# Layer 1's first eight maxima moved into the last two expert tiles of layer 0, and its second batch's queries spread over steps 1 to 4

## The chip, the cores and the metric

The kernel runs on one NeuronCore of a Trainium2 chip. Its engines are TensorE (PE in the profile; its weight loads are PEld), VectorE (DVE), ScalarE (ACT), GpSimd (POOL) and SyncE (SP, which here only issues DMAs). The trace counts a float32 matmul as two instructions. Each works through its own instructions in order and waits on semaphores for the others. The metric is the device time of one execution in microseconds; lower is better.

## The reference, cut to what matters

Two layers of cross attention and a mixture of experts, in float32, for x of 2 x 512 x 256 and a context of 2 x 1024 x 256:

```python
x = x + xattn0(layernorm(x), ctx, ctx, mask0)       # 16 heads of 16
x = x + experts0(layernorm(x))                      # top 1 of 8, 256 -> 512 (gelu) -> 256, cosine routing
x = x + xattn1(layernorm(x), ctx, ctx, mask1)       # q, k, v are each layer-normed after their projection
x = x + experts1(layernorm(x))                      # shared + top 2 of 7, 256 -> 704 -> 256
# in xattn1:
q = layer_norm(query @ Wq, gq, bq); k = layer_norm(key @ Wk, gk, bk); v = layer_norm(value @ Wv, gv, bv)
weights = softmax(q @ k.T / sqrt(16) + bias)        # per head, per batch element
out = weights @ v
```

The masks leave only the last 256 keys to be attended to in the rows that matter, so the fast way of the kernel works on 256 keys.

## The kernel before, in words

**Attention.** The work of a layer is eight steps n: batch element n // 4, four of the 16 heads (group n % 4). Each step has eight units of scores (`pe_scores`, units i = 0 to 7): two 32 x 128 by 256 matmuls into one bank of PSUM, head i % 4 in its own 32 rows of the array, queries of half i // 4. VectorE takes the row maxima of each unit (`dve_top`, L956) into NM. When the eight are done, TensorE turns NM (`pe_turn_max`, L783), VectorE adds it to the queries (`dve_add_max`, L962), so that the weights come out with their maximum taken off. Then TensorE computes eight units of weights, transposed (`pe_weights`, L774), ScalarE takes their Exp (L1084), TensorE multiplies with the values (`pe_outputs`, L795, two halves), and two steps later turns the outputs (`pe_turn_out`, L808), which VectorE divides (`dve_divide`). The maxima run ahead of the weights: while step n's weights are made, units 4 to 7 of step n + 1 and 0 to 3 of step n + 2 are scored. A step has four gaps with two units of weights and two of scores each; beside each gap stands a list of other jobs (`pe_beside`, `dve_beside`, `act_beside`).

**PSUM.** Scores go round banks 0 to 2 (m, freed by VectorE), weights and the jobs beside round banks 3 to 5 (e, freed by ScalarE), banks 6 and 7 are claimed by name (`claim`, `taken`). The order of uses is a table (`ring_uses`, `BESIDE_M`, `BESIDE_E`, `bank_uses`).

**Layer 0's experts.** Sixteen tiles of 128 tokens (`ffn0_pe`, L1603 up, L1614 down, L1616 bias), in the order: turn of the next tile's rows (L1591), up(i), mid(i), down(i - 1), beside(i); after the last tile down(15). Up goes to banks 0 and 1 in turn, the turned rows to bank 2, down to banks 3 and 4. ScalarE does Gelu (L1644) and takes the outputs out (`take_y`, L1635), SP stores them to DRAM; GpSimd gathers them back into token order.

**Before layer 1's first step.** For the first batch element: combine the gathered rows into x (L994), the statistics of the layer norm (L395 to L408: moments, their aggregation, an inverse root in small steps), normal rows (x1_0, by ScalarE in beside(12)), their turn (`turn_batch`, beside(13)), the projection to queries (`project_batch`, L364, beside(14)), the statistics and norms of these (q1_0, L430 and L434), then behind the expert tiles the turns by heads (`turned_heads`, L349) in `second_pe`, which ScalarE takes with scale and bias (`queries_out`, L624), and then `pe_first(1)`: units 0 to 7 of step 0 and 0 to 3 of step 1, while VectorE does the maxima. Behind the last expert tile every engine has a branch (`fork`) that reads whether any expert got more rows than its main tiles hold.

**The second batch element's queries.** VectorE combines and takes the statistics of x1_1 between the maxima of `pe_first(1)` (`queries_begun`), ScalarE norms them before its first Exp, TensorE turns them in step 0, gap 0, and projects in gap 2; statistics of q1_1 in step 1 between the maxima, norms at step 1, gap 3, then one turn by heads at gap 3 of each of steps 1 to 4.

## Time and profile before

| | us |
|---|---|
| median of 3 runs (545.52 to 547.08) | 546.33 |
| the profiled execution | 548.11 |
| its span | 546.9 |
| TensorE busy | 504.9 (92%) |
| VectorE busy | 261.6 (48%) |
| ScalarE busy | 207.3 (38%) |
| mean granted TensorE clock | 0.967 of full |

In the time of the span, layer 0's attention runs to about 140, its experts to 219.6, layer 1's attention to about 325, the shared expert to about 389, the routed experts to the end. The profile's slices of the granted clock are below full in two places: at about 125 to 132 and from 218 to 276.

### The profile page before, as it was taken

Reading aid. Unit: us, or ns where it says so; the run is one execution under the profiler, and the core shown is the slowest. Engines: PE = TensorE matmul, PEld = TensorE weight load, DVE = VectorE, ACT = ScalarE, POOL = GpSimd, SP = SyncE. Lnnn points to the kernel's source line nnn. Section 1 sums busy time; section 2 is a strip of 40 time slices with the busy share of each in tenths; the row PEclk is TensorE's granted clock in tenths of the full one; section 3 lists DMA queues with packets and bytes.
Section 4 is the critical chain, followed back from the end, with each engine's and each line's share of the span. In section 5 each row is a group of like instructions: output and inputs, shape, how many; then the busy total and the mean of one; then the engine's idle time right before and its main releaser. Section 6 shows DMA issues by size and latency. Waiting matters only on the chain.

```text
span 546.9 us, 8791 instructions
## 1 busy us (share of the span) xinstructions
PE 504.9 (92%) x3285; PEld 373.3 (68%) x3285; DVE 261.6 (48%) x789; ACT 207.3 (38%) x425; POOL 82.2 (15%) x108
## 2 busy tenths in 40 slices
PE   2999999999889999679699998999999999999995
PEld 1456555645778999546356435656799999999994
DVE  5567798673337364365577826161322222222220
ACT  2434645462346653225466662220122222222221
POOL 2400700002102110200000000017212122212222
PEclk9999999997999999859899999999999999999999
DMA  8500005997113230380000012009786677666712
GB/s 299 188 1 0 2 1 164 369 373 224 59 38 104 72 97 20 99 296 1 0 2 2 1 39 77 1 10 362 269 282 201 202 238 248 211 200 220 251 13 33
DMA packets 42435, 72.06 MB, mean 132 GB/s; under 512 B 3405, under 2 KB 33037, under 8 KB 42384
## 3 DMA queue, kind: packets, MB, share of 16 engines
q1 hardware_dynamic: 33648, 60.65, 32.5%
q0 software_dynamic: 4336, 6.75, 5.6%
q10 hardware_dynamic: 4400, 4.01, 2.3%
q8 instruction: 29, 0.48, 0.3%
q14 instruction: 22, 0.18, 0.1%
HBM read 56.88 MB, written 14.51 MB: 131 GB/s over the span
## 4 chain that ended last, share of the span: by engine, by line
PE 57%; DVE 5%; DMA 3%; issue 2%; ACT 1%; POOL 1%; POOLq 0%; ACTq 0%; DVEq 0%
PE PS L1817 16%; PE PS L1832 9%; PE PS L1726 6%; PE PS L764 4%; PE PS L774 4%; PE PS L1737 3%; PE PS L1614 3%; PE PS L1603 3%; PE PS L795 2%; DVE W L956 2%; DMA VR<-scratch_rows 1%; PE PS L364 1%; PE PS L349 1%; PE PS L333 1%; PE PS L808 1%
## 5 line engine op out<-in xcount | busy, mean ns | idle before, releaser
L956 DVE TENSOR_REDUCE W<-PS 128x2 f32<-128x512 f32 x128 | 84.7, 687 | 41.3 <-PE PS L764 40.6
L1817 PE MATMUL PS<-PR,W 128*128 128x128 f32 x836 | 96.5, 275 | 0.0
L1817 PEld LDWEIGHTS PS<-PR,W 128*128 128x128 f32 x836 | 94.9, 192 | 0.1
L764 PE MATMUL PS<-W 32*128 32x256 f32 x512 | 85.7, 432 | 3.1 <-issue 1.6
L774 PE MATMUL PS<-W 32*128 32x512 f32 x256 | 84.3, 672 | 0.7 <-ACT W L1084 0.7
L764 PEld LDWEIGHTS PS<-W 32*128 32x128 f32 x512 | 56.4, 201 | 18.5 <-DVE W L956 9.0
L1832 PE MATMUL PS<-W,PR 128*128 x228 | 52.5, 380 | 0.8 <-ACT PR L2461 0.8
L2512 POOL DMA_INDIRECT out<-PR,slots x19 | 29.6, 1560 | 128.6 <-ACT PR L2461 125.4
L1084 ACT ACTIVATE PR<-PS 128x512 f32<-128x512 f32 x64 | 34.9, 595 | 30.8 <-PE PS L774 30.6
L1832 PEld LDWEIGHTS PS<-W,PR 128*128 128x128 f32 x228 | 41.9, 190 | 6.1 <-issue 1.2
L1084 ACT ACTIVATE W<-PS 128x512 f32<-128x512 f32 x64 | 34.7, 595 | 24.0 <-PE PS L774 24.0
L1853 DVE TENSOR_TENSOR PR<-PR,PS 128x512 f32<-128x512 f32 x19 | 13.1, 688 | 59.8 <-PE PS L1817 59.8
L1726 PE MATMUL PS<-XT,W 128*128 128x512 f32 x88 | 40.1, 596 | 0.0
L774 PEld LDWEIGHTS PS<-W 32*128 32x128 f32 x256 | 26.0, 191 | 19.5 <-issue 6.7
L1603 PE MATMUL PS<-PR,W 128*128 128x128 f32 x256 | 31.2, 275 | 0.0
L1614 PE MATMUL PS<-W,PR 128*128 128x256 f32 x128 | 30.4, 381 | 0.0
L1603 PEld LDWEIGHTS PS<-PR,W 128*128 128x128 f32 x256 | 29.9, 192 | 0.1
L1726 PEld LDWEIGHTS PS<-XT,W 128*128 128x128 f32 x88 | 16.2, 190 | 16.5 <-issue 16.1
L1644 ACT ACTIVATE PR<-PS,b1c 128x128 f32<-128x128 f32 x64 | 18.2, 366 | 23.8 <-PE PS L1603 23.8
L1614 PEld LDWEIGHTS PS<-W,PR 128*128 128x128 f32 x128 | 23.1, 190 | 2.6
L1566 POOL DMA_INDIRECT scratch_rows<-CT,posi x8 | 7.8, 969 | 113.5 <-DVE posi L1530 111.4
L1737 PEld LDWEIGHTS PS<-W,PR 128*128 128x128 f32 x96 | 18.1, 190 | 8.7 <-issue 4.5
(260 smaller groups left out, 625.5 us busy)
## 6 DMA issues: line engine op xcount, KB each, us to landing
W<-in_rguT SPq DMA_DIRECT2D x19, 1408.0 KB, 6.1
W<-in_L_ffn_W SPq DMA_DIRECT2D x16, 512.0 KB, 9.6
W<-in_rdT SPq DMA_DIRECT2D x5, 768.0 KB, 9.5
W<-in_mask SPq DMA_DIRECT2D x3, 1024.0 KB, 14.3
scratch_rows<-W SPq DMA_DIRECT2D x1, 2860.0 KB, 14.8
VR<-scratch_rows SPq DMA_DIRECT2D x19, 130.0 KB, 5.3
scratch_x<-W SPq DMA_DIRECT2D x1, 2048.0 KB, 14.1
PR<-scratch_x SPq DMA_DIRECT2D x16, 128.0 KB, 2.2
```

The lines of the kernel that those rows point to most:

```text
L764: m = pe.matmul(PS[:, bank, q * FK:(q + 1) * FK], QT[r:r + 32, g, c:c + 128], KT[r:r + 32, g, b * FK:(b + 1) * FK], start=True, stop=True)
L774: pe.matmul(PS[:, bank, :], KT[r:r + 32, g, b * FK + kb * 128:b * FK + (kb + 1) * 128], QT[r:r + 32, g, 512 * b:512 * (b + 1)], start=True ...
L956: dve.tensor_reduce(NM[:, s % 2, q:q + 2, c], PS[:, m_bank(use), :].rearrange("p (q n) -> p q n", q=2), AX, ALU.max).then_inc(sem("m_free" ...
L1084: act.activation(PX[s % 2][:, HEADS_W[k], :], PS[:, e_bank(use), :], ACT.Exp).then_inc(sem("e_free"), 1)
L1603: m = pe.matmul(PS[:, i % 2, j * 128:(j + 1) * 128], W[:, o:o + 128], XS0[:, i % 2, k, :], start=(k == 0), stop=(k == 1))
L1614: pe.matmul(PS[:, bk, 0:D], HT0[:, i % 2, j, :], W[:, o:o + D], start=(j == 0), stop=False)
L1644: act.activation(HT0[:, i % 2, j, :], PS[:, i % 2, j * 128:(j + 1) * 128], ACT.Gelu, bias=b1c[:, c:c + 1]).then_inc(sem("gelu"), 1)
L1726: m = pe.matmul(PS[:, 2 * (n % 2) + w, :], W[:, k * 2 * F1 + o:k * 2 * F1 + o + 128], XT[:, k, 512 * b:512 * b + 512], start=(k == 0), sto ...
L1737: m = pe.matmul(half(4 + t // 2, t), HS[:, n % 2, t * 128:(t + 1) * 128], W[:, o:o + D], start=(j == 0 and t % 2 == 0), stop=(j == NJ1 - 1 ...
L1817: m = pe.matmul(PS[:, bank, j * 128:(j + 1) * 128], W[:, o:o + 128], XS[:, r % 2, k, :], start=(k == 0), stop=(k == 1))
L1832: m = pe.matmul(PS[:, 6, 0:D], HT[:, r % 2, j, :], W[:, bass.ds(slot * SLOT + o, D)], start=(j == 0), stop=(j == NJ1 - 1))
L2512: ins = pool.indirect_dma_start(out, off, YO[:, r % 2, :], None, compute_op=ALU.add)
```

## The change

- **Inside the expert tiles** (`fast_...`, `ffn0_...`): VectorE norms two of the four rows of x1_0 and ScalarE two, in tile 11; the turn moves to beside(12), the projection to mid(13), the norms of q1_0 into tile 13, the four turns by heads to beside(14) (two) and mid(15) (two). The up matmuls swap banks 0 and 1 (`up_bank`).
- **First eight maxima:** units 0 to 7 of layer 1's step 0 are issued in pairs: in the middle of up(15), in the middle of down(14), in beside(15), in the middle of down(15). Units 0 to 3 of step 1 and the turned maxima follow the last tile, ahead of the branch.
- **Second batch's queries:** the combine runs in step 0 from gap 2; the statistics of x1_1 stand as one block before step 1's maxima; norms at step 1, gap 0; turn at gap 1; projection at gap 3; statistics of q1_1 in step 2, two pieces per maximum; its norms at step 3, gap 0; the turns by heads at step 3, gaps 0, 1 and 3, and step 4, gap 3.
- **Scores of steps 4 and 5:** units 0 to 3 of step 4, which need these queries, move from step 2 to step 3: none in step 2, gaps 2 and 3, and step 3, gap 0, then four in each of gaps 1, 2 and 3 of step 3; the turned maxima of step 4 move to the end of gap 3.
- The way for overfull experts (`again_...`, left out here) recomputes what the tiles now hold.

In the diff below many of the removed lines are left out; they stand in the functions printed above.

```diff
-    BESIDE_E = {(0, 5, 1): ["close0_0"], (0, 7, 1): ["rows0_0_0"], (1, 0, 0): ["x1_1_0"], (1, 0, 2): ["q1_1_0", "q1_1_1"]}
-    BESIDE_E.update({(1, 1 + g, 3): [f"q1t1_{g}"] for g in range(NG)})
+                (0, 7, 1): ["rows0_0_1"], (1, 1, 1): ["x1_1_1"]}
+    BESIDE_E = {(0, 5, 1): ["close0_0"], (0, 7, 1): ["rows0_0_0"], (1, 1, 1): ["x1_1_0"], (1, 1, 3): ["q1_1_0", "q1_1_1"],
+                (1, 3, 0): ["q1t1_0"], (1, 3, 1): ["q1t1_1"], (1, 3, 3): ["q1t1_2"], (1, 4, 3): ["q1t1_3"]}
+    def tops_of(l, n, gap):
+        if (l, n, gap) in ((1, 2, 2), (1, 2, 3), (1, 3, 0)):
+            return []
+        if (l, n) == (1, 3):
+            return [(4, i) for i in range(4 * gap - 4, 4 * gap)] if gap < 3 else [(5, i) for i in range(4)]
+        s, first = (n + 1, 4 + 2 * gap) if gap < 2 else (n + 2, 2 * gap - 4)
+        return [(s, i) for i in (first, first + 1) if s < STEPS]
...
         else:
+            if (n, gap) == (1, 1):
                 pe.wait_ge(sem("x1_rows"), 8)
                 turn_ring("x1_1", rows_for(0, 1))
+            elif (n, gap) == (1, 3):
                 pe.wait_ge(*e_freed("x1_1_0"))
                 pe.wait_ge(*m_freed("x1_1_1"))
                 for j in range(2):
                     project_half(e_claim(f"q1_1_{j}"), j, 2, 1).then_inc(sem("e_full"), 1)
+            elif (n, gap) == (3, 0):
+                pe.wait_ge(sem("q1_rows"), 4)
+                turned_heads(e_claim("q1t1_0"), RB[1], 0).then_inc(sem("e_full"), 1)
+            elif (n, gap) == (3, 1):
+                turned_heads(e_claim("q1t1_1"), RB[1], 1).then_inc(sem("e_full"), 1)
+            elif n in (3, 4) and gap == 3:
                 turned_heads(e_claim(f"q1t1_{n - 1}"), RB[1], n - 1).then_inc(sem("e_full"), 1)
...
+    def pe_pairs(l, n, gap):
+        tops = tops_of(l, n, gap)
+        if gap % 2:
+            pe_weights(l, n, 2 * gap)
+            pe_weights(l, n, 2 * gap + 1)
+            for s, i in tops:
+                pe_scores(l, s, i)
+            return
+        for k in range(2):
+            for s, i in tops[k:k + 1]:
+                pe_scores(l, s, i)
+            pe_weights(l, n, 2 * gap + k)
+        for s, i in tops[2:]:
+            pe_scores(l, s, i)
     def pe_step(l, n):
+        pe_pairs(l, n, 0)
         pe_turn_out(l, n - 2)
         pe_beside(l, n, 0)
+        pe_pairs(l, n, 1)
         pe_outputs(l, n - 1, 1)
         pe_beside(l, n, 1)
+        pe_pairs(l, n, 2)
+        if (l, n) != (1, 3):
+            pe_turn_max(l, n + 1)
         pe_beside(l, n, 2)
+        pe_pairs(l, n, 3)
+        if (l, n) == (1, 3):
+            pe_turn_max(l, n + 1)
         if n == STEPS - 1:
             pe_turn_out(l, n - 1)
         pe_outputs(l, n, 0)
...
+    def dve_step(l, n, v, late, pieces=1, since=0):
         for gap in range(4):
+            tops = tops_of(l, n, gap)
+            for k, (s, i) in enumerate(tops):
+                if gap == 1 and n > 1 and k == len(tops) - 1:
                     dve_divide(l, n - 2, v)
+                dve_top(l, s, i)
+                if gap >= since:
+                    for _ in range(pieces):
+                        next(late, None)
+            if gap == 1 and n > 1 and not tops:
+                dve_divide(l, n - 2, v)
+            if gap == (3 if (l, n) == (1, 3) else 2) and n + 1 < STEPS:
                 dve_add_max(l, n + 1)
...
     def act_beside(l, n, gap):
...
+            if (n, gap) == (1, 0):
+                act_x1(1)
+            elif (n, gap) == (1, 1):
                 act_xt_ring("x1_1", 1)
+            elif (n, gap) == (1, 3):
                 for j in range(2):
...
+            elif (n, gap) == (3, 0):
+                act.wait_ge(sem("stats"), NORMS[True]["q1_1"])
+                act.wait_ge(sem("wz"), 16)
+                for j in range(4):
+                    normal_act("q1_1", j, heads(RB[1][:, j, :]), by_head(RW[:, j, :])).then_inc(sem("q1_rows"), 1)
+                act_late_queries(0)
+            elif (n, gap) == (3, 1):
+                act_late_queries(1)
+            elif n in (3, 4) and gap == 3:
+                act_late_queries(n - 1)
             elif (n, gap) == (7, 1):
                 rows_taken_act(1, 0)
...
-    def ffn0_pe(tiles, beside, mid=lambda i: None):
+    def up_bank(i):
+        return (i + 1) % 2
...
+                if j == NJ0 // 2:
+                    half(i, "up")
                 for k in range(2):
                     o = expert(i) + k * F0 + j * 128
-                    m = pe.matmul(PS[:, i % 2, j * 128:(j + 1) * 128], W[:, o:o + 128], XS0[:, i % 2, k, :],
+                    m = pe.matmul(PS[:, up_bank(i), j * 128:(j + 1) * 128], W[:, o:o + 128], XS0[:, i % 2, k, :],
                                   start=(k == 0), stop=(k == 1))
             m.then_inc(sem("up"), 1)
...
             for j in range(NJ0):
+                if j == NJ0 // 2:
+                    half(i, "down")
                 o = expert(i) + 2 * F0 + j * D
...
                 ranks_pe(1).then_inc(sem("ranks"), 1)
+            elif i == 13:
+                pe.wait_ge(sem("wp_2"), 16)
+                project_batch("q1_0", "x1_0", 2, 0)
+            elif i == 15:
+                claim(7, "q1t0_2")
+                filled(7, turned_heads(7, RB[0], 2))
+                pe.wait_ge(*at(1, "qt", 1))
+                turned_heads(5, RB[0], 3).then_inc(sem("q_ps"), 1)
+        def first_maxima(i, part):
+            if (i, part) == (15, "up"):
+                pe.wait_ge(*at(1, "qt", 1))
+                pe.wait_ge(*at(1, "masked", 1))
+                pe.wait_ge(sem("gelu"), NJ0 * 15)
+                pe_scores(1, 0, 0)
+                pe_scores(1, 0, 1)
+            elif (i, part) == (14, "down"):
+                pe.wait_ge(sem("gelu"), NJ0 * 16)
+                pe_scores(1, 0, 2)
+                pe_scores(1, 0, 3)
+            elif (i, part) == (15, "down"):
+                pe_scores(1, 0, 6)
+                pe_scores(1, 0, 7)
         def beside(i):
...
-            elif i == 13:
+            elif i == 12:
                 pe.wait_ge(sem("x1_rows"), 4)
                 turn_batch("x1_0", rows_for(0, 0))
...
             elif i == 14:
+                taken(6, "q1_0")
+                taken(7, "q1_0")
+                turned_heads(5, RB[0], 0).then_inc(sem("q_ps"), 1)
+                claim(6, "q1t0_1")
+                filled(6, turned_heads(6, RB[0], 1))
+            elif i == 15:
+                pe_scores(1, 0, 4)
+                pe_scores(1, 0, 5)
+        ffn0_pe(MAIN, beside, mid, first_maxima)
+        pe.wait_ge(*at(1, "masked", 4))
+        pe.wait_ge(*at(1, "qt", 2))
+        taken(6, "q1t0_1")
+        taken(7, "q1t0_2")
+        pe_scores(1, 1, 0)
+        pe_scores(1, 1, 1)
+        pe_turn_max(1, 0)
+        pe_scores(1, 1, 2)
+        pe_scores(1, 1, 3)
         fork(pe, 0)
...
+        pe.wait_ge(sem("y_out"), TILES0)
+        pe.wait_ge(sem("vv1"), 4)
...
+            elif i == 10:
+                for n in range(3):
+                    dve.wait_ge(*at(1, "kt", n + 1))
+                    mask_keys(1, n)
             elif i == 11:
                 dve.wait_ge(sem("kept"), 16)
                 whole(combine(v, 0))
                 whole(statistics(v, "x1_0", rows_of(0)))
+                for j in range(2):
+                    normal_dve("x1_0", j, OB[:, 0, j, :], X[:, j, :]).then_inc(sem("x1_rows"), 1)
             elif i == 12:
+                dve_xt("x1_0", 0)
             elif i == 13:
                 raw = [half(6 + j // 2, j) for j in range(4)]
                 whole(statistics(v, "q1_0", raw, True, [full(6 + j // 2, "q1_0") for j in range(4)]))
+                dve.wait_ge(sem("pads"), 3)
+                normal_dve("q1_0", 2, heads(RB[0][:, 2, :]), by_head(half(7, 2))).then_inc(*v.up())
+                freed(7, normal_dve("q1_0", 3, heads(RB[0][:, 3, :]), by_head(half(7, 3))))
+            elif i == 14:
+                dve.wait_ge(*at(1, "kt", 4))
+                mask_keys(1, 3)
+            elif i == 15:
+                dve_first(1, nothing)
...
+            late = begun if s < 2 else queries_norm() if s == 2 else rows_early() if s == 6 else empty
+            if s == 0:
+                dve_step(1, s, v, late, 1, 2)
+                continue
+            if s == 1:
+                whole(late)
+            dve_step(1, s, v, late, 2 if s == 2 else 1)
             whole(late)
             if s == 5:
...
+            elif i == 11:
+                act.wait_ge(sem("stats"), NORMS[True]["x1_0"])
+                for j in (2, 3):
+                    normal_act("x1_0", j, OB[:, 0, j, :], X[:, j, :]).then_inc(sem("x1_rows"), 1)
             elif i == 12:
+                act_xt("x1_0", (6,), 0)
             elif i == 13:
+                act.wait_ge(sem("stats"), NORMS[True]["q1_0"])
+                act.wait_ge(sem("pads"), 3)
+                normal_act("q1_0", 0, heads(RB[0][:, 0, :]), by_head(half(6, 0))).then_inc(sem("q1_half"), 1)
+                freed(6, normal_act("q1_0", 1, heads(RB[0][:, 1, :]), by_head(half(6, 1))))
+            elif i == 14:
+                queries_out(1, 0, 5).then_inc(sem("qt"), 1)
+                act.wait_ge(*full(6, "q1t0_1"))
+                freed(6, queries_turned(1, 0, 1, 6))
+            elif i == 15:
+                act.wait_ge(*full(7, "q1t0_2"))
+                freed(7, queries_turned(1, 0, 2, 7))
+                act.wait_ge(*at(1, "q_ps", 2))
+                queries_turned(1, 0, 3, 5).then_inc(sem("qt"), 1)
```

## Rows read from the trace of the kernel before

**Rows 1.** The page's part 4: shares of the span in the chain, by engine.

```profile
PE 57%; DVE 5%; DMA 3%; issue 2%; ACT 1%; POOL 1%; POOLq 0%; ACTq 0%; DVEq 0%
```

**Rows 2.** The chain that ended last, 200 to 300: start, us, what.

```profile
210.67 3.46 PE PS L364 x16
...
219.58 2.22 issue
...
280.78 0.59 PE PS L349 x4
...
288.35 0.99 PE PS L795 x8
289.34 0.59 PE PS L349 x4
```

**Rows 3.** Windows: busy us (count) of PE, PEld, DVE, ACT, POOL; clock; DMA share, GB/s.

```profile
50.00:52.00 2.00, 1.94 (x18) 1.15 (x17) 1.98 (x5) 0.72 (x2) 0.00 (x0) 1.00 0.00 0
...
219.58:289.86 70.28, 56.85 (x378) 37.35 (x377) 41.59 (x100) 31.98 (x56) 4.00 (x6) 0.81 0.23 76
226.00:228.00 2.00, 1.27 (x13) 0.84 (x8) 1.49 (x3) 0.00 (x0) 0.95 (x1) 0.90 0.33 86
228.00:230.00 2.00, 2.00 (x12) 1.81 (x11) 1.35 (x3) 0.00 (x0) 0.00 (x0) 0.50 0.17 53
...
248.00:250.00 2.00, 2.00 (x20) 1.61 (x14) 1.30 (x3) 1.58 (x3) 0.00 (x0) 0.98 0.00 0
...
268.00:270.00 2.00, 0.23 (x1) 0.23 (x2) 0.00 (x0) 1.72 (x4) 0.00 (x0) 0.64 0.00 0
...
274.00:276.00 2.00, 2.00 (x16) 1.27 (x20) 0.39 (x2) 0.26 (x2) 0.00 (x0) 0.65 0.00 0
```

**Rows 4.** Timeline of TensorE: start, us, line, form, count, idle before it.

```profile
201.94 0.38 PE L1591 MATMUL PS<-ident,PR 128*128 128x128 f32 x2
...
225.38 1.15 PE L764 MATMUL PS<-W 32*128 32x256 f32 x12 [1.61 <-issue]
...
244.51 1.97 PE L333 MATMUL PS<-ident,W 128*128 128x128 f32 x8 [3.75 <-ACT W L434]
...
269.77 1.11 PE L349 MATMUL PS<-ident,W 128*128 128x128 f32 x4 [5.10 <-ACT W L434]
```

**Rows 5.** Timeline of VectorE.

```profile
195.02 1.66 DVE L994 SCALAR_TENSOR_TENSOR X<-W,gw,X 128x256 f32<-128x256 f32 x4
196.71 1.41 DVE L395 BATCH_NORM_STATS2 ST<-X 128x6 f32<-128x256 f32 x4
...
200.81 0.16 DVE L408 SCALAR_TENSOR_TENSOR NW<-MV,NW 128x4 f32<-128x4 f32 x1
...
217.82 1.00 DVE L430 TENSOR_SCALAR W<-PS,MV,NW 128x256 f32<-128x256 f32 x2
226.51 1.89 DVE L956 TENSOR_REDUCE W<-PS 128x2 f32<-128x512 f32 x3 [7.70 <-PE PS L764]
```

**Rows 6.** Timeline of ScalarE.

```profile
219.90 1.02 ACT L434 ACTIVATE W<-PS,NW 128x256 f32<-128x256 f32 x2
...
244.47 1.28 ACT L1084 ACT_TABLE_LOAD   x1
...
267.65 2.07 ACT L434 ACTIVATE W<-W,NW 128x256 f32<-128x256 f32 x4 [3.15 <-DVE NW L408]
```

**Rows 7.** Timeline of TensorE in layer 0's opening.

```profile
38.02 1.14 PE L764 MATMUL PS<-W 32*128 32x256 f32 x8
39.09 1.98 PE L344 MATMUL PS<-XT,W 128*128 128x512 f32 x4
```

**Rows 8.** Timeline of all engines, GpSimd's gathers and SP's last store.

```profile
220.03 0.32 SPq L1688 DMA_DIRECT2D scratch_y<-PR  x1
...
222.46 0.94 POOL L1675 DMA_INDIRECT W<-scratch_y,posi  x1 [29.33 <-DMA scratch_y<-PR]
...
226.20 0.95 POOL L1675 DMA_INDIRECT W<-scratch_y,posi  x1 [0.30 <-issue]
```

More of the change, by code:

```diff
@@ L271, in ring_uses @@
             for n in range(STEPS):
-                tops = [("top", l, n + 1, i) for i in range(4, 8)] + [("top", l, n + 2, i) for i in range(4)]
                 for gap in range(4):
-                    m += [top for top in tops[2 * gap:2 * gap + 2] if top[2] < STEPS]
+                    m += [("top", l, s, i) for s, i in tops_of(l, n, gap)]
                     m += BESIDE_M.get((l, n, gap), [])
@@ L1002, in queries_begun, with dve_first @@
         yield from statistics(v, "x1_1", rows_of(1))
-    def dve_first(l, beside, late=iter(())):
+    def dve_first(l, beside):
         for i in range(8):
@@ L1035, in dve_beside @@
         else:
-            if (n, gap) == (0, 0):
+            if (n, gap) == (1, 1):
                 dve_xt_ring("x1_1", 1)
@@ L1039, in dve_beside @@
                 rows_taken_dve(1, 0)
-    def dve_step(l, n, v, late):
+    def dve_step(l, n, v, late, pieces=1, since=0):
         for gap in range(4):
-            s, first = (n + 1, 4 + 2 * gap) if gap < 2 else (n + 2, 2 * gap - 4)
-            for i in (first, first + 1):
-                if s < STEPS:
-                    dve_top(l, s, i)
-                    next(late, None)
-                if gap == 1 and i == 6 and n > 1:
-                    dve_divide(l, n - 2, v)
-            if gap == 2 and n + 1 < STEPS:
+            tops = tops_of(l, n, gap)
+            for k, (s, i) in enumerate(tops):
+                if gap == 1 and n > 1 and k == len(tops) - 1:
+                    dve_divide(l, n - 2, v)
+                dve_top(l, s, i)
[5 more added lines that the diff above has]
+            if gap == (3 if (l, n) == (1, 3) else 2) and n + 1 < STEPS:
                 dve_add_max(l, n + 1)
@@ L1154, in act_beside @@
                                    ).then_inc(sem("e_free"), 1)
-            elif 1 <= n < 5 and gap == 3:
-                if n == 1:
-                    act.wait_ge(sem("stats"), NORMS[True]["q1_1"])
-                    act.wait_ge(sem("wz"), 16)
-                    for j in range(4):
-                        normal_act("q1_1", j, heads(RB[1][:, j, :]), by_head(RW[:, j, :])).then_inc(sem("q1_rows"), 1)
-                use = f"q1t1_{n - 1}"
-                act.wait_ge(*e_full(use))
-                queries_turned(1, 1, n - 1, e_bank(use)).then_inc(sem("e_free"), 1)
+            elif (n, gap) == (3, 0):
[8 more added lines that the diff above has]
+                act_late_queries(n - 1)
             elif (n, gap) == (7, 1):
@@ L1582, in expert, with ffn0_pe @@
         return (i % E0) * EXP0
-    def ffn0_pe(tiles, beside, mid=lambda i: None):
+    def up_bank(i):
+        return (i + 1) % 2
+    def ffn0_pe(tiles, beside, mid=lambda i: None, half=lambda i, part: None):
         def turn_x(i):
@@ L2094, in again_dve @@
         whole(statistics(v, "q1_0", [half(6 + j // 2, j) for j in range(4)], "again"))
+        dve.wait_ge(sem("again_xt"), 2 + NG)
+        turns = 2 + NG
+        for n in range(12):
+            g, i = n // 8, n % 8
+            if n == 10:
+                turns += 1
+                dve.wait_ge(sem("again_turned"), turns)
+                qt = QT[:, 0, 0:512]
+                dve.tensor_tensor(qt, qt, PS[:, 7, :], ALU.add).then_inc(sem("again_xt"), 1)
+            turns += 1
+            dve.wait_ge(sem("again_turned"), turns)
+            q, c = 2 * (i // 4), 32 * (i % 4) + ROW_MAX
+            dve.tensor_reduce(NM[:, g, q:q + 2, c], PS[:, 0, :].rearrange("p (q n) -> p q n", q=2), AX, ALU.max
+                              ).then_inc(sem("again_xt"), 1)
     def second_dve(v):
         empty = iter(())
-        late = queries_begun(v)
-        def beside(i):
-            if i > 2:
-                next(late, None)
         def queries_norm():
@@ L2110, in rows_early @@
             yield from dve_rows(1, 0)
-        dve_first(1, beside, late)
-        whole(late)
+        begun = queries_begun(v)
         for s in range(8):
-            late = queries_norm() if s == 1 else rows_early() if s == 6 else empty
-            dve_step(1, s, v, late)
+            late = begun if s < 2 else queries_norm() if s == 2 else rows_early() if s == 6 else empty
[5 more added lines that the diff above has]
+            dve_step(1, s, v, late, 2 if s == 2 else 1)
             whole(late)
@@ L2179, in fast_act @@
         ffn0_act(MAIN, beside)
-        act.wait_ge(sem("stats"), NORMS[True]["q1_0"])
-        for j in range(2):
-            ins = normal_act("q1_0", j, heads(RB[0][:, j, :]), by_head(half(6, j)))
-            if j == 0:
-                ins.then_inc(sem("q1_half"), 1)
-        freed(6, ins)
         fork(act, 2)
```

126 lines of the change are left out of this document (43 added, 83 removed).

## The prediction

> **What bounds the kernel now.** I read first the chain that ended last: TensorE holds 57% of the span [rows 1], so the kernel is bound by the order of TensorE's work and by what it waits for. The stretch that the diff touches lies between the end of layer 0's last expert tile (219.58, where the chain goes over into issue) and the first weights of layer 1's step 4 (289.9, right behind the turned heads at 289.34 [rows 2]). I then read the windows [rows 3]: 70.28 us at a mean granted clock of 0.81. A step at full clock takes 8.56 us (280.78 to 289.34 [rows 2]). So the four steps would be worth some 34 us, and the stretch holds twice that.
>
> TensorE's timeline shows why [rows 4]. It stands 2.22 us for the query norm and the branch [rows 2], 1.61 us for ScalarE to take the turned queries, 3.75 us for the norm of x1_1 (a four-row statistic that VectorE does between maxima, then 2.07 us of ScalarE [rows 6]), and 5.10 us for the norm of q1_1 in step 1. The granted clock falls from 1.00 to 0.50 (2.4 to 1.2 GHz) after the first two of these gaps and some small matmuls, at about 227.8, and returns at about 248.0; it falls again at about 268.7, four microseconds into the 5.10 us gap, and returns at about 275.3 [rows 3]. That is 27 us at half clock.
>
> The opening (12 maxima, 227 to 240) is bound half by VectorE (1.89 for three maxima [rows 5]) and half by the slow clock; nothing else lies beside it.
>
> **The change part by part.** Times below are on the trace's own axis.
>
> *First queries.* The norms of x1_0 are split (two on VectorE, two on ScalarE), the turn moves to tile 12, the projection to tile 13, the four turns of heads to tiles 14 and 15. TensorE's amount does not change; where the work stood after the tiles it now stands within them. Check of the cover: the statistics end at 200.97 (last instruction at 200.81 [rows 5]), two norms each on both engines until 202.0; TensorE asks at 201.94: nothing. The projection ended at 214.13 (210.67 + 3.46 [rows 2]) and VectorE's two norms at 218.82 (217.82 + 1.00 [rows 5]), 4.7 us later; until beside(14) TensorE now has down(12), a turn of x, up(14) and down(13), the same work as up(15) and the two downs after the projection now (214.13 to 219.58, 5.45) and 0.2 more: 5.7. Cost 0; if the cover is 1 us short it is 1 us. On ScalarE the Gelus of tile 14 start 0.7 us late; down(14) asks for them 4 us later. The masks move one to two tiles earlier into idle time of VectorE.
>
> *Eight maxima in pairs.* A pair of scores between full matmuls costs 1.07 us in layer 0 (38.02 to 39.09 [rows 7]) at full clock. Bounds: 0.77 (three scores took 1.15 at 225.38 [rows 4], two thirds of it) to 2.1 (half clock). I take 1.07, the same form. Four pairs 4.3, and 1.96 for the turned heads that before ran at 221.80: the tiles end at 219.58 + 6.3 = 225.9. VectorE's two maxima (1.29) hide under the half downs of 0.9 and the next pair. The ring of three banks gives each score its bank in time (score 7 wants the fourth maximum's, free at about 223.4, and asks at 224.4).
>
> *Opening.* Two pairs and the turned maxima: 2 x 1.07 + 0.59 = 2.7, so 228.6. The branch then costs TensorE about 0.85: before, the norm ends at 220.92 [rows 6] and TensorE starts at 221.80 (219.58 + 2.22 [rows 2]). VectorE's branch, hidden before under 7.70 idle [rows 5], is now open: its last maxima end at 229.9, it goes on at 230.8. Bounds for each branch: 0.05 to 2.2 (the whole gap). ScalarE's wait for the last store of y, now ahead of the first Exp: the take-out of tile 15 ends at 226.5, 2.4 us to landing (220.03 to 222.46 [rows 8]): 228.9, not late. The load of the Exp table (1.28 [rows 6]) may come after the first weights: 0 to 1.3; taken 1.3, and VectorE's lag hides part, so 0.8.
>
> *Step 0.* VectorE bounds it: 230.8 + 8 maxima at 0.65 in a run (5.2) + 0.7 for the added maxima + 1.66 for the four combines [rows 5] + 0.8 = 239.2. The gathers that these want are issued from 228.9 at 1.24 apart [rows 8], the fourth at 232.6; the fourth is asked for at about 238.5, and lateness is possible only if a gather takes over 5 us; 0 to 1 us, taken 0. TensorE finishes its step at 237.1. The weight loads on SP's queue wait for the same gathers and come 6 to 7 us later; they have 80 us before they are used, cost 0.
>
> *Step 1.* All of x1_1's statistic now stands as one block ahead of VectorE's maxima: 4.26 (196.71 to 200.97 [rows 5]), until 243.5. Behind it on VectorE wait the maxima of (2,4) to (2,7), and on those TensorE, whose ring is full at 239.4. It stands until 244.2, 4.8 us. ScalarE's norms run 243.5 to 245.6, later than its step-1 Exps 0 and 1, earlier than its 2 and 3. A gap of 4.8 has its like in the 5.10 gap, where the clock fell; so half clock from about 244 to 248 (from 244.51 it took 3.4 us to return, from 269.77 5.5 [rows 3, 4]): bounds 0 to 5.5 us low, 0 to 3 us of cost; taken 2.4. Outputs 1.95 and the turn of x1_1 1.97 at half clock, then two pair blocks, turned maxima, outputs (1.0) and the projection (3.46): 255.9. So step 1 costs 18.8 from 237.1.
>
> *Step 2.* It has four maxima where a steady step has eight. q1_1's statistic goes in two pieces per maximum. VectorE from 256.6: four maxima 2.8, four moments 1.5, aggregates and first steps 0.9, divide 0.7, giving 262.5 for the last maximum, where TensorE wants it at 260.6: 1.9 us of wait (bounds 0 to 3). The step ends at 265.0, 9.1 us.
>
> *Step 3.* The norm of q1_1 stands here: weights 0.9, turned outputs 0.6, then ScalarE's two Exps and 2.07 of norms: TensorE stands from 266.5 to 269.05, 2.55 us instead of 5.10. ScalarE must take the first turned group before score (4,0) may start (0.8; the last of four cost TensorE the gap of 1.61 [rows 4]). Then twelve maxima in three gaps bound VectorE: 12 x 0.68 + 0.67 divide + 0.69 = 9.6, from 271.0 to 280.6. So step 3 costs 15.6 against 8.56; its bounds are 12 (TensorE's own work and the wait) and 18 (a second fall of the clock).
>
> Step 4 begins at 280.6 instead of 289.9. From there the orders are the same, every later time moves along, and the load of the last weights is tied to step 7's end as before. Sum: +6.3 at the tiles, then 54.7 us (225.9 to 280.6) where 70.3 stood: 9.3 us gained. The profiled execution took 548.11 (span 546.9), so 538.8; the median of the runs is 1.8 below it, so **537.0**.
>
> One rule is weighed here. TensorE is busy for all of 228 to 230 with scores alone, and the clock stays at 0.50 [rows 3]; in layer 0's first step, as thin and also behind VectorE, it is 1.00 (50 to 52 [rows 3]). The Trainium skill (TensorE: Matmul & The Clock Gate, section A second HAM failure mode: psum-queue depth-cycling) says that short idle moments between groups of matmuls, as banks are waited for, can make the clock swing although no pause is long. By that rule steps 0 and 3 run low, which is rival B; by layer 0's row they do not.
>
> **The rivals.**
>
> *A, the lumps hide better.* The branch shows on neither engine, the clock stays at full through step 1, the ring lets step 2 run as TensorE's work: 1.7 + 2.4 + 1 less, so 533.7, median 532. For it: layer 0's first step at 1.00; the wait of 3.75 did not occur at full clock, so its limit is not seen. Against it: the fall inside the 5.10 gap.
>
> *B, the clock falls in the steps that VectorE paces.* From about 229 to 250 and in step 3. Step 0 then costs TensorE four pair blocks of 2.1, 2.0, 1.1 and 1.3 = 12.8 instead of 9.9 at VectorE's pace, +2.5; step 3's scores, outputs and turned heads, 4.2 at full clock, take 7: +2.8. Total 5.3, so 544.1, median 542.3. For it: 227.8 to 248.0 in this trace, with like work. Against it: between halves of expert tiles full matmuls stand, which is how layer 0 ran its first eight maxima [rows 7].
>
> *C, the other side.* One mechanism: having fallen at the branch, the clock never returns before step 4, because waits for VectorE break up each step. TensorE's work from 229.4 to 280.6 at full clock is 16 blocks of 1.07, 7 outputs of 0.99 (288.35 [rows 2]), 8 turns of 0.59, a turn of 0.99 and 3.46 = 33; at half 66, and with the two norm waits (about 7.4) 73 instead of 51.2: 22 more, 12.7 slower than before, 560.8, median 559. It decides from the point where over 9.3 us of extra time, so 19 us of that work instead of some 4, runs at half clock. For it: 20 us in a row now. Against it: the clock returned at 248.0 and at 275.3 within ordinary steps.
>
> **How the numbers follow.** Chances: forecast 0.45, A 0.18, B 0.26, C 0.05, and 0.06 for a wait that I have not seen and that eats the gain. A measurement here tells about 0.3%, 1.6 us, from no change. The bounds of the terms (pairs, branches, step 1's clock, step 2's wait, step 3) give the forecast's own case 533.5 to 541; to leave out no more than 2 in 10 the range takes A's centre and B's far side: 532 to 544. Faster: forecast, A, B and a little of the rest, 0.88; same 0.05; slower 0.07.
>
> **What would show it.** Right: the last expert tile's matmuls end at 225 to 227; TensorE's granted clock is 1.00 there; the gap before the turn of x1_1 is 3 to 5 us with VectorE's statistic in it; the gap before the first turned q1_1 heads is 2 to 3 us; step 4 begins at 278 to 284; everything behind is of the same length. Wrong: a gap ahead of beside(12) or beside(14) over 1 us (first queries not covered), half clock from 229 on (B, C), or a statistic of x1_1 that waits for its gathers.

## The result, and the profile after

| | us |
|---|---|
| kernel after, median of 8 runs (549.2 to 553.04) | 550.85 |
| kernel before, median of 8 runs (545.52 to 549.29) | 546.88 |
| ratio, 95% interval | 1.0072 [1.0047, 1.0098] |
| profiled execution of after, its span | 552.44, 551.2 |
| mean granted TensorE clock | 0.964 |

The change makes the kernel slower by 0.7%, 4.0 us. The prediction was 537.0 with a range of 532 to 544 and a chance of 0.88 for faster: wrong in sign. Three single runs below (two of fill3_table0, one of sooner_split) lie over 1.5% above the fastest of their kernel, with a lower mean clock, and the medians and ratios leave them out.

The chain of waits of after begins its shares with this line; TensorE holds 58% of the span where it held 57% [rows 1].

```profile
PE 58%; DVE 6%; ACT 2%; DMA 2%; issue 1%; POOL 1%; ACTq 0%; POOLq 0%; DVEq 0%
```

The two traces first have to be laid on one axis. In this window of unchanged code the kernel before ran at a mean clock of 0.58:

```profile
124.00:132.00 8.00, 8.00 (x43) 2.82 (x42) 2.74 (x17) 1.44 (x3) 0.00 (x0) 0.58 1.01 298
```

The windows of after follow: the window, TensorE's and its weight loads' busy time, that of VectorE, ScalarE and GpSimd, and behind them the mean granted clock, the share of the DMA engines and GB/s. The first is the same stretch at 1.00, so after's axis runs 8 x 0.42 = 3.4 us ahead from there on.

```profile
124.00:132.00 8.00, 8.00 (x54) 4.88 (x53) 4.79 (x23) 1.80 (x4) 2.22 (x3) 1.00 0.98 298
225.80:293.77 67.97, 59.45 (x308) 33.11 (x306) 35.21 (x89) 27.80 (x49) 3.82 (x6) 0.72 0.23 76
226.00:228.00 2.00, 1.54 (x13) 0.89 (x10) 1.98 (x4) 0.98 (x1) 1.51 (x2) 1.00 0.24 66
225.80:238.83 13.03, 11.61 (x61) 6.33 (x59) 8.14 (x15) 5.74 (x9) 3.60 (x4) 0.61 0.57 190
268.00:270.00 2.00, 0.02 (x1) 0.02 (x1) 0.00 (x0) 1.93 (x4) 0.00 (x0) 0.91 0.01 4
265.73:293.77 28.04, 24.83 (x104) 13.82 (x100) 9.12 (x15) 8.63 (x16) 0.00 (x0) 0.57 0.01 1
280.00:282.00 2.00, 2.00 (x13) 1.47 (x15) 0.00 (x0) 1.03 (x2) 0.00 (x0) 0.50 0.00 0
292.00:294.00 2.00, 2.00 (x16) 0.92 (x12) 0.00 (x0) 0.12 (x1) 0.00 (x0) 0.62 0.05 8
```

The window from the first weights to step 4 answers to the 0.81 window of [rows 3]: its clock is 0.72. TensorE's timeline gives the places (the steps begin at 225.80, 238.83, 256.57, 265.73 and 293.77):

```profile
212.19 1.14 PE L775 MATMUL PS<-W 32*128 32x256 f32 x8
...
222.69 1.14 PE L775 MATMUL PS<-W 32*128 32x256 f32 x8
223.76 0.66 PE L794 MATMUL PS<-ident,W 128*128 128x128 f32 x4
...
225.80 0.69 PE L785 MATMUL PS<-W 32*128 32x512 f32 x1
...
228.96 1.22 PE L785 MATMUL PS<-W 32*128 32x512 f32 x1 [1.42 <-ACT PR L1090]
...
238.83 0.51 PE L775 MATMUL PS<-W 32*128 32x256 f32 x1
...
244.30 1.12 PE L775 MATMUL PS<-W 32*128 32x256 f32 x4 [2.46 <-DVE W L963]
...
256.57 0.48 PE L775 MATMUL PS<-W 32*128 32x256 f32 x1
...
263.09 0.66 PE L794 MATMUL PS<-ident,W 128*128 128x128 f32 x4 [1.43 <-DVE W L963]
263.68 1.13 PE L785 MATMUL PS<-W 32*128 32x512 f32 x4
264.74 1.07 PE L806 MATMUL PS<-PR,VR 128*32 128x512 f32 x8
265.73 1.13 PE L785 MATMUL PS<-W 32*128 32x512 f32 x4
...
269.98 1.11 PE L360 MATMUL PS<-ident,W 128*128 128x128 f32 x4 [2.53 <-ACT W L445]
...
284.86 5.20 PE L775 MATMUL PS<-W 32*128 32x256 f32 x17
...
293.77 0.48 PE L775 MATMUL PS<-W 32*128 32x256 f32 x1
```

Step 3 is 28.04 us long against 15.6 forecast, at a mean clock of 0.57. VectorE, which was to bound it, is idle for long stretches there, as its own timeline of after shows (the number in brackets is the idle time before):

```profile
225.06 0.68 DVE L969 TENSOR_TENSOR W<-W,PS 128x512 f32<-128x512 f32 x1
225.66 2.60 DVE L963 TENSOR_REDUCE W<-PS 128x2 f32<-128x512 f32 x4
...
274.91 1.89 DVE L963 TENSOR_REDUCE W<-PS 128x2 f32<-128x512 f32 x3 [9.44 <-PE PS L775]
...
282.68 1.29 DVE L963 TENSOR_REDUCE W<-PS 128x2 f32<-128x512 f32 x2 [4.22 <-PE PS L775]
```

### The profile page after: what moved, and what is told of

Its sections match the earlier page's. It is cut to its first block, busy times and chain, and to the rows that moved or that the text cites. A ratio compares the mean times of both kernels' runs of the same rounds, so it can differ in the third digit from the quotient of the medians.

```text
span 551.2 us, 8794 instructions
## 1 busy us (share of the span) xinstructions
PE 512.9 (93%) x3285; PEld 374.8 (68%) x3285; DVE 263.7 (48%) x791; ACT 206.0 (37%) x423; POOL 82.6 (15%) x108
## 4 chain that ended last, share of the span: by engine, by line
PE 58%; DVE 6%; ACT 2%; DMA 2%; issue 1%; POOL 1%; ACTq 0%; POOLq 0%; DVEq 0%
PE PS L1838 17%; PE PS L1853 8%; PE PS L1747 6%; PE PS L775 5%; PE PS L785 4%; PE PS L1758 3%; PE PS L1635 3%; PE PS L806 3%; PE PS L1622 2%; DVE W L963 2%; PE PS L375 1%; PE PS L360 1%; PE PS L794 1%; DVE ST L406 1%; PE PS L344 1%
## 5 line engine op out<-in xcount | busy, mean ns | idle before, releaser
L775 PE MATMUL PS<-W 32*128 32x256 f32 x512 | 89.0, 437 | 4.3 <-DVE W L963 3.5
L785 PE MATMUL PS<-W 32*128 32x512 f32 x256 | 86.4, 682 | 2.2 <-ACT PR L1090 1.4
L775 PEld LDWEIGHTS PS<-W 32*128 32x128 f32 x512 | 57.5, 204 | 29.5 <-DVE W L963 14.1
L785 PEld LDWEIGHTS PS<-W 32*128 32x128 f32 x256 | 26.3, 195 | 15.4 <-issue 6.5
L1665 ACT ACTIVATE PR<-PS,b1c 128x128 f32<-128x128 f32 x64 | 18.2, 366 | 19.6 <-PE PS L1622 19.6
```

What stands on the lines that cost most here:

```text
L775: m = pe.matmul(PS[:, bank, q * FK:(q + 1) * FK], QT[r:r + 32, g, c:c + 128], KT[r:r + 32, g, b * FK:(b + 1) * FK], start=True, stop=True)
L785: pe.matmul(PS[:, bank, :], KT[r:r + 32, g, b * FK + kb * 128:b * FK + (kb + 1) * 128], QT[r:r + 32, g, 512 * b:512 * (b + 1)], start=True ...
L1665: act.activation(HT0[:, i % 2, j, :], PS[:, up_bank(i), j * 128:(j + 1) * 128], ACT.Gelu, bias=b1c[:, c:c + 1]).then_inc(sem("gelu"), 1)
```

## The experiments

Four kernels ran on one chip (kernel before there 548.21), four on a second (547.95), two on a third (549.28). Ratios are to the kernel before on the same chip; the kernel after itself was timed only against the 546.88 above, so it is compared with the others by ratio. The theory: step 3's thin work (scores alone, and a wait) holds the clock at half and is TensorE's own cost. The rivals: the fall in step 0, the Exp table, or the first half of the change.

**fill3**: dense work in step 3's wait.

```diff
+    def fill(bank, n):
+        for _ in range(n):
+            pe.matmul(PS[:, bank, :], ident[:, :], XT[:, 0, 0:512], start=True, stop=True)
...
             elif (n, gap) == (3, 0):
+                bank = e_claim("q1t1_0")
+                fill(bank, 3)
                 pe.wait_ge(sem("q1_rows"), 4)
-                turned_heads(e_claim("q1t1_0"), RB[1], 0).then_inc(sem("e_full"), 1)
+                turned_heads(bank, RB[1], 0).then_inc(sem("e_full"), 1)
```

> The changed kernel, with three full 128x512 matmuls (results overwritten, so nothing of the output depends on them) issued by TensorE ahead of its wait for the normed q1_1 rows in step 3. Theory W (the 2.5 us wait makes the clock fall, and the score blocks behind it then run at half clock): with the wait filled the clock stays at 1.00 through step 3, which takes 15 to 17 us instead of 28; about 11 to 12 us less than the changed kernel's 550.9, so 539. Rival S (the score blocks themselves are too thin and lose the clock, wait or not): the clock falls some us later inside step 3, gain 0 to 5 us, 546 to 551. Rival V (VectorE's twelve maxima pace step 3, the clock is only a symptom): no change, 549 to 553.

Measured: 546.61 (543.73 to 548.77, 10 runs), ratio 0.9968 [0.9933, 1.0003]; profiled 544.54, clock 0.986. TensorE's timeline of this kernel:

```profile
265.78 1.13 PE L785 MATMUL PS<-W 32*128 32x512 f32 x4
...
267.34 2.74 PE L861 MATMUL PS<-XT,ident 128*128 128x512 f32 x6
270.03 0.66 PE L360 MATMUL PS<-ident,W 128*128 128x128 f32 x4
...
271.58 1.14 PE L775 MATMUL PS<-W 32*128 32x256 f32 x12
273.54 1.13 PE L775 MATMUL PS<-W 32*128 32x256 f32 x4 [0.81 <-DVE W L969]
...
278.84 3.16 PE L775 MATMUL PS<-W 32*128 32x256 f32 x17
...
282.51 1.91 PE L806 MATMUL PS<-W,VR 128*32 128x512 f32 x8
...
285.40 0.76 PE L775 MATMUL PS<-W 32*128 32x256 f32 x1
```

The same step, the same thin work, at full clock until 282.6: 19.6 us, of which some 1.4 are the half clock at its end (outputs 1.91 for 1.0, turned heads 1.12 for 0.6). That divides the 28.04 of after, as an estimate: 18.2 of work and waits, 9.8 of clock. The mean clock of all ten runs is 0.978 to 0.988, where after's eight have 0.964 to 0.972, so the higher clock shows in every run and not in this one alone. By ratio (1.0072 to 0.9968) it is worth some 5.7 us.

That is half of what theory W said: the median lies in the range of rival S (546 to 551) and not at 539. The clock did fall once more in step 3, at 282.6, behind bare scores, and the last wait before that was the 0.81 us at 273.54. The profiled execution also had no fall in step 0, where nothing was changed, so its 544.54 is not the fill's work alone. VectorE's timeline of it shows what paces the step at full clock:

```profile
272.79 1.89 DVE L969 TENSOR_REDUCE W<-PS 128x2 f32<-128x512 f32 x3 [7.26 <-PE PS L775]
...
277.34 2.60 DVE L969 TENSOR_REDUCE W<-PS 128x2 f32<-128x512 f32 x4 [1.44 <-PE PS L775]
280.12 2.60 DVE L969 TENSOR_REDUCE W<-PS 128x2 f32<-128x512 f32 x4 [0.18 <-PE PS L775]
```

**late_fill**: dense work, four such matmuls, behind the first four scores of step 3 (bank of `q1t1_1`).

> The changed kernel, with four full 128x512 matmuls behind the first four scores of step 3 (gap 1), the wait for q1_1 left bare. The clock falls in the wait as before. Theory S (score blocks keep the clock low because they load little of the array): dense matmuls bring it back, the clock is 1.00 from about 282 instead of 293; the fill costs about 7 us at half clock and gives back about 5 to 6: 550 to 553, with step 3's gaps 2 and 3 at full clock. Theory W in its strict form (once lost, any busy TensorE returns after the same time, and this stretch just took long): no return before 290 and the 7 us of fill on top: 556 to 558.

Measured: 553.85 (6 runs), ratio 1.0119 [1.0075, 1.0163]; profiled 555.31. The median lies at the upper end of what theory S said (550 to 553), below W's 556 to 558, and the trace decides for neither. In this execution the clock fell at 263.1, at the wait at step 2's end, and stayed at half until 287.0; it returned 4.3 us after the dense matmuls began, but table0, which has none, returned at 287.2 from a fall at 266.7. So dense work behind the wait bought no time (after's ratio is 1.0072) and took 5.83 us, mostly at half clock; whether it brought the clock back isn't shown. TensorE's timeline and the windows of late_fill:

```profile
263.07 1.10 PE L794 MATMUL PS<-ident,W 128*128 128x128 f32 x4 [1.43 <-DVE W L969]
...
282.70 5.83 PE L861 MATMUL PS<-XT,ident 128*128 128x512 f32 x8
```

```profile
280.00:282.00 2.00, 2.00 (x11) 0.38 (x9) 1.26 (x3) 0.00 (x0) 0.00 (x0) 0.50 0.00 0
286.00:288.00 2.00, 2.00 (x5) 0.78 (x4) 0.00 (x0) 0.00 (x0) 0.00 (x0) 0.74 0.00 0
288.00:290.00 2.00, 2.00 (x19) 1.30 (x18) 0.00 (x0) 0.78 (x1) 0.00 (x0) 1.00 0.00 0
```

**table0**: ScalarE loads the Exp table ahead of its wait for the store.

```diff
     def second_act():
+        act.activation(junk[:, :], one8[:, 0:1], ACT.Exp)
         stored(act, TILES0)
```

> The changed kernel with the Exp table loaded on ScalarE by one small Exp right behind the branch, ahead of the wait for the stores, instead of at the first weights. TensorE's gap of 1.42 us in step 0 goes. If that gap is what made the clock fall at about 228.7, step 0 takes about 9.5 us instead of 13 and the time falls by 3 to 4 us (547). If the thin opening alone does it, only the gap goes: 0 to 1.5 us less (549.5 to 551).

Measured: 547.28 (10 runs), ratio 0.9995 [0.9961, 1.0029]; profiled 552.12. The median is the 547 expected if that gap makes the clock fall. In the profiled execution step 0 has neither the gap of 1.42 nor a fall and takes 7.6 us (231.68 to 239.26), but the clock falls at 246.3 (behind a gap of 3.47) and again from 266.7 to 287.2, and the time is that of after's. The quickest runs of this kernel (544.4, clock 0.978) lack some of that. Its timeline of ScalarE shows the load ahead of the first Exp:

```profile
229.31 1.28 ACT L2306 ACT_TABLE_LOAD   x1 [0.24 <-issue]
```

**second_only**: the second half of the change on the kernel before, with the opening behind the expert tiles.

> Only the second half of the change: the second batch's queries as jobs of steps 1 to 4 with the scores of step 4 in step 3, while the first twelve maxima stay behind the expert tiles as in the kernel before. If the first half is worth what the traces of both kernels show (18.1 us from the tiles' end to the first weights before, against 3.2 and 6.3 more in the tiles now), this kernel is 8 to 9 us slower than the changed one: 558 to 561. If the first half gives nothing of its own because the clock takes it back, it is 549 to 552.

Measured: 562.17 (4 runs), ratio 1.0272 [1.0227, 1.0318]; profiled 559.98, half clock at 220.4 to 251.1, 258 to 261.4 and 282 to 295.5. The second half by itself costs 15 us (2.7% of 548.21, 14.9), 1 us more than the first case of the expectation. Its step 3, the same code behind the same wait of 2.53, took 23.7 us (277.97 to 301.67) and not 28.0: there the clock was back after 13.7 us.

**first_only**: the first half, with the second batch's queries where the kernel before has them.

```diff
             if s == 0:
-                dve_step(1, s, v, late, 1, 2)
-                continue
-            if s == 1:
-                whole(late)
-            dve_step(1, s, v, late, 2 if s == 2 else 1)
+                whole(begun)
+            dve_step(1, s, v, late)
```

> The kernel after with its second half taken back: maxima in the last expert tiles, but the second batch's queries in the places of the kernel before (turn of x1_1 at step 0 gap 0, projection at gap 2, statistics of q1_1 in step 1, norms at step 1 gap 3, turns by heads in steps 1 to 4, scores always beside weights). The combine and the statistics of x1_1 stand as one block ahead of step 0's maxima, since the tiles leave VectorE no place for them. If the two halves are independent terms, this kernel is 15 us quicker than the changed one (second half alone against the kernel before: +15 us): about 536. If the second half is what makes room for the first (the gathers can't start before the last store of y, so that their 4 gathers, 1.7 of combine, 4.3 of statistics and 2.1 of norms stand open behind the tiles), TensorE stands some 12 to 15 us at step 0 gap 0, the clock falls there, and the time is 545 to 552; step 3 is then an ordinary one of 8.5 to 9 us at full clock.

Measured: 549.77 (10 runs), ratio 1.0001 [0.997, 1.0031]. The second case of the expectation holds, with a wait of 11.77 us for the 12 to 15 said. TensorE's timeline:

```profile
245.05 1.33 PE L339 MATMUL PS<-ident,W 128*128 128x128 f32 x5 [11.77 <-ACT W L440]
```

and VectorE's, where the gathers of the last tiles' rows come first:

```profile
234.15 0.48 DVE L990 SCALAR_TENSOR_TENSOR X<-W,gw,X 128x256 f32<-128x256 f32 x1 [1.46 <-DMA W<-scratch_y,posi]
...
238.54 1.41 DVE L401 BATCH_NORM_STATS2 ST<-X 128x6 f32<-128x256 f32 x4
```

The halves are no independent terms: first alone 0, second alone +15, both +4. What the first half saves in the opening it gives back as a wait for rows that the second half covers.

**fill3_table0**: both edits.

> The changed kernel with both single edits: three full matmuls ahead of the wait in step 3, and the Exp table loaded ahead. If the two losses are separate, their gains add: 1.0 percent and 0.7 percent less than the changed kernel, 0.989 to 0.992 of the kernel before. If they are one and the same (either keeps the clock by shifting when it is looked at), no more than the better of the two: 0.996 to 1.000.

Measured: 542.45 (539.86 to 545.92, 7 runs), ratio 0.9907 [0.9874, 0.9939]; profiled 542.45, half clock in this stretch only from 240.8 to 247.6. The two gains add, as the first case said. With steps 0 and 3 at full clock after's loss is gone, and some 5 us more. TensorE's timeline of it has both steps at a clock of 1.00 from end to end, step 0 from 228.46 to 236.05 and step 3 from 264.73 to 283.05, so 7.6 and 18.3 us:

```profile
228.46 0.69 PE L785 MATMUL PS<-W 32*128 32x512 f32 x1
...
236.05 0.48 PE L775 MATMUL PS<-W 32*128 32x256 f32 x1
...
264.73 1.13 PE L785 MATMUL PS<-W 32*128 32x512 f32 x4
...
283.05 0.48 PE L775 MATMUL PS<-W 32*128 32x256 f32 x1
```

**sooner**: the same first half, but the norm of q1_1 comes a step earlier and the scores of steps 4 and 5 go back to their gaps beside weights.

```diff
-                (1, 3, 0): ["q1t1_0"], (1, 3, 1): ["q1t1_1"], (1, 3, 3): ["q1t1_2"], (1, 4, 3): ["q1t1_3"]}
+                (1, 2, 1): ["q1t1_0"], (1, 2, 3): ["q1t1_1"], (1, 3, 3): ["q1t1_2"], (1, 4, 3): ["q1t1_3"]}
...
-        if (l, n, gap) in ((1, 2, 2), (1, 2, 3), (1, 3, 0)):
-            return []
-        if (l, n) == (1, 3):
-            return [(4, i) for i in range(4 * gap - 4, 4 * gap)] if gap < 3 else [(5, i) for i in range(4)]
```

The projection moves to step 1, gap 2, its statistics begin there, the norms stand at step 2, gap 0.

> The changed kernel with the second half of the change drawn together so that no block of scores stands alone: projection of q1_1 at step 1 gap 2 instead of 3, its statistics from there, norms at step 2 gap 0 (ScalarE), the turned heads at step 2 gap 1 and 3, step 3 gap 3, step 4 gap 3, and the scores of steps 4 and 5 back in their usual gaps beside weights. The first half is kept. Theory L (the twelve scores of step 3 without weights beside them are the loss: they cost TensorE some 6 us by themselves and hold the clock at half when it has fallen): steps 2 and 3 take 18 to 20 us instead of 37, the clock falls in them for less than 8 us; 0.970 to 0.975 of the kernel before. Rival W (the norm waits alone decide, the scores' place does not matter): one wait of 2 us remains, the clock falls in it as before and is low for some 20 us; 0.995 to 1.005 of the kernel before.

Measured: 539.18 (536.76 to 541.15, 4 runs), ratio 0.9852 [0.9817, 0.9888]; profiled 536.76, clock 0.986, half clock in this stretch only from 243.7 to 250.6. TensorE's timeline of it (many rows left out):

```profile
257.51 0.69 PE L781 MATMUL PS<-W 32*128 32x512 f32 x1
...
258.62 0.66 PE L815 MATMUL PS<-ident,W 128*128 128x128 f32 x4
...
261.61 1.13 PE L771 MATMUL PS<-W 32*128 32x256 f32 x4 [1.12 <-DVE W L955]
...
269.74 0.48 PE L771 MATMUL PS<-W 32*128 32x256 f32 x1
...
278.25 0.48 PE L771 MATMUL PS<-W 32*128 32x256 f32 x1
```

Steps 2 and 3 took 12.2 and 8.5 us (257.50, 269.74, 278.25), 20.7 together, which is just above the 18 to 20 of theory L. After has 9.2 and 28.0, and at full clock it would have 9.2 and the 18.3 of fill3_table0: so some 7 us are the order of the work and 10 the clock. The ratio of 0.9852 lies between theory L (0.970 to 0.975) and rival W (0.995 to 1.005), and as this kernel changes both the wait and the scores' place, it doesn't part the two.

Two units of weights with two of scores in turn with them took 1.11 (257.51 to 258.62). In after two units of weights alone took 1.06 (263.68 to 264.74), and with two of scores behind them 1.30 (258.24 to 259.54): leaving two scores out saves 0.05 to 0.24. Two units of scores alone take 1.07. In fill3 three took 1.14 (the x12 at 271.58), and the fourth, which waited for one of the three banks, another 1.13.

**sooner_split**: as sooner, the norms shared by ScalarE and VectorE.

> As the kernel with the scores back in their usual gaps, and the norms of x1_1 and q1_1 split between ScalarE and VectorE, two rows each. By the path each norm is 1.0 us shorter (2.07 to 1.05), of which VectorE's maxima take part back: 0 to 2 us less than without the split, the clock falls less often in the waits. If VectorE is what TensorE waits for, it is 0 to 1 us more.

Measured: 540.45 (537.97 to 541.00, 3 runs), ratio 0.9841 [0.9803, 0.9879]. No gain over sooner can be told, where 0 to 2 us were expected.

**sooner_all**: as sooner_split, with the early table and two dense matmuls ahead of the turned heads.

> Scores in their usual gaps, norms split, Exp table loaded ahead, and two full matmuls ahead of the wait for q1_1's rows at step 2 gap 1. If the clock is the rest of the loss there: 0.962 to 0.970 of the kernel before, with a granted clock at 1.00 in steps 2 and 3. If the fill only lengthens TensorE's path: 0 to 2 us more than the split alone.

Measured: 539.25 (4 runs), ratio 0.9837 [0.9812, 0.9861]. The 0.962 to 0.970 was missed: the profiled execution (540.2) was at half clock from 243.7 to 250.5 and from 264.2 to 267.6, behind waits of 4.12 and 1.77 us, so that the clock of steps 2 and 3 was not yet full.

**sooner_fill**: as sooner, with three dense matmuls in the wait of step 1.

```diff
             pe_weights(l, n, 2 * gap + 1)
+            if (l, n, gap) == (1, 1, 1):
+                fill(e_claim("x1_1_0"), 3)
             for s, i in tops:
```

> The kernel with the norm in step 2, and three full 128x512 matmuls (six records, 2.7 us) behind the weights of step 1 gap 1, ahead of the scores that wait 3.47 us for VectorE's statistic of x1_1. If a wait that follows thin work lets the clock fall and dense matmuls in it keep it up, the half clock from 243.9 to 251.7 goes: outputs 1.94 to 1.07, turn 1.97 to 1.07, two pairs 0.9 less each, some 3 us in all, so a ratio of about 0.980 to the kernel before (536 to 537). If only the amount of idle time counts, the fill changes that too (3.47 to about 0.8), and the time is the same; so this run doesn't tell these two apart, but it tells both from a third: that the clock falls in the step whatever stands in the wait (then 539 to 540, no gain).

Measured: 540.51 (4 runs), ratio 0.9819 [0.9754, 0.9885]. Step 1 kept its full clock, but this execution was at half clock from 229.6, by a gap of 1.42 at which sooner had not fallen, to 239.8, and from 260.3 to 270.6. So the expectation, a ratio of 0.980 against no gain, is not decided: the four kernels' intervals overlap. They are all 1.5 to 1.8% faster than before, and faster than both kernels of this case.

## Why the prediction was wrong

The forecast on after's axis (3.4 us less than in the text), against the measured lengths:

| step of the prediction | forecast | measured |
|---|---|---|
| *first queries*, tiles' end | 222.5 | 222.7 |
| *eight maxima in pairs* | 1.07 each | 1.07 |
| *opening* to the first weights, a branch with it | 3.55 | 3.1 |
| *step 0* on TensorE | 7.65 | 13.0 |
| *step 1* | 18.8 | 17.7 |
| *step 2* | 9.1 | 9.2 |
| *step 3* | 15.6 | 28.0 |

The forecast sum was a gain of 9.3. The rows differ by +0.2, -0.4, +5.4, -1.1, +0.1 and +12.4, together 16.6: a loss of 7.3 in this pair of executions, as 552.44 - 548.11 + 3.4 = 7.7 says; the medians give 4.0, since after's profiled execution, at a mean clock of 0.964, lies near the top of its runs.

- **The step that failed is *step 3*,** 15.6 against 28.0. The larger error in it is the clock, put at nothing in the sum and at one short fall in the bound of 18. In the pair of executions it cost 9.7 us: the same step took 18.3 at full clock (fill3_table0), and in after the clock was at half from 269.6 to 293.5 (by the windows at 0.91 and 0.62). In that time TensorE and not VectorE set the pace; VectorE stood idle 9.44 and 4.22 us.
- **The smaller error in *step 3*** is 2.7 us at full clock. "Twelve maxima in three gaps bound VectorE" is nearly so there: in fill3 VectorE waits only 0.18 us between the last two runs of four. But its first maximum came 7.0 us behind the step's begin where 6.0 stood, from there to the added maxima it took 10.5 where 9.6 stood, as it waits 1.44 us for scores, and TensorE's outputs and turned heads end 0.8 later. TensorE's work in the step was never summed; scores without weights beside them are not free. The scores taken out of step 2 saved 0.3 us there.
- ***Step 0*** took rival B's way and price on TensorE (12.8 told, 13.0 measured). At full clock and without a wait for the table it takes the 7.6 us that the forecast had (table0, fill3_table0), in sooner with the wait and at full clock 8.9 (229.01 to 237.87). So of the 5.4 us some 1.3 are the gap of 1.42 for the Exp table, which came where it was put, and some 4.2 the clock: it fell in that gap and stayed at half from 228.7 to 238.9. In before it was at half there as well, from 227.6 by the row at 0.90 and not from 227.8 as the prediction reads it [rows 3]. Taking only this gap away (table0) brings after to before's time; with the fill of step 3 it is 0.9% faster than before.
- **Rival B** was priced at 5.3 us for both steps. Its step 0 was right on TensorE (over steps 0 and 1 the forecast was short by 4.3; B said 2.5, though its own figures, 12.8 and 9.9, differ by 2.9), its step 3 (+2.8) counted only scores, outputs and turned heads and not the bare weights and waits. **Rival C**, half clock to step 4, had the right kind of place but not its length: steps 1 and 2 ran mostly at full clock.
- **What held:** the cover of the first queries, the pairs in the tiles, step 2. *Step 1* held in its length and not in its parts: its terms add up to 18.2 and not 18.8, its wait was 2.46 where 4.8 stood, because TensorE came to it late out of step 0, and the scores of 1.06 behind the wait were not in the sum. The wait of *step 3* was 2.53 for 2.55. The branches, taken at 0.85 for each engine, show on neither: TensorE goes from the last scores to the weights at 225.80, VectorE makes four maxima in a run from 225.66, two on each side of its branch; that much of rival A was so.
- **The rule weighed** in the prediction is borne out in part. The clock was at 0.50 in a window with TensorE busy for all 2.00 us (280 to 282), and it fell in or just behind waits of 1.42, 2.46 and 2.53 us for the table, a statistic and a norm. The Trainium skill (TensorE: Matmul & The Clock Gate, section A second HAM failure mode: psum-queue depth-cycling) names frequent short idle moments between groups of matmuls as a cause of a swinging clock. The trace agrees in so far as none of these waits is long; they are single waits, though, and the fall at 282.6 in fill3 has none near it. I set the rule against one row of layer 0 at 1.00 [rows 3] and gave it 0.26; that row has no wait over 0.8 us in the 20 us ahead of it, and fill3 ran most of step 3 that way at 1.00 as well.

Open stays why the same gap is followed by a fall in one execution and not in another. In the stretch of these steps every wait of 2.29 us or longer that began at full clock held a fall or was followed by one within 1.8 us, in all twelve traces. The shorter ones went either way. At the gap of step 0 (1.42 to 1.43) the clock fell in after, late_fill and sooner_fill, 1.5 us behind it in sooner_split, and not in fill3 and sooner; at the one at step 2's end (1.43 to 1.44) it fell in late_fill and table0 and not in after, fill3, fill3_table0 and second_only. The dip near 124 to 132, in code that no kernel here changes, is in before, fill3, sooner, sooner_split and first_only, for half as long in table0, and not in after; TensorE's timeline of before shows no wait from 116 to 141, so the clock falls without one too. The seven runs of fill3_table0 spread over 6.1 us, with mean clocks from 0.992 (539.86) to 0.979 (545.92): one profile is no measure of a term that is clock. What brings the clock back is open too: behind the same wait it took 23.9 us in after and 13.7 in second_only.

## What to carry to other kernels

Ask of each small matmul what it stands beside: two quarter-height units of scores next to two of weights cost 0.05 to 0.24 us, alone 1.07, so moving it to make a wait shorter can cost more than the wait. Then ask what clock the stretch behind each wait runs at: a wait of 2.5 us ahead of thin work cost 10 us in one execution and 5 in another (23.7 against 18.3), and three dense matmuls in that wait took some 6 us off the typical run. For a step's forecast sum the work of every engine, also where one seems to bound, and add what they wait for each other.

## What was not expected of the hardware

- The clock stayed at 0.50 for 23.9 us with TensorE busy for nearly all of them (269.6 to 293.5 in after), as long in late_fill, and for 20.5 in table0.
- The same step ran at 1.00 (fill3) up to 282.6 when 2.74 us of dense matmuls stood in place of the 2.53 us wait, and in fill3_table0 to its end.
- Two units of scores between the halves of an expert tile cost 1.07 us, and beside two units of weights 0.05 to 0.24.
- The clock fell at 282.6 in fill3 and at 125.2 in before with no wait of TensorE over 0.81 us in the 9 us ahead.
- The branches of TensorE and VectorE behind the expert tiles showed no time in the trace.
